# Head mixing on four 64x64 tiles of TensorE: exponentials moved unscaled, with their sums in an extra column, and mixing weights scaled per row by GpSimd

## What is computed

```python
dots = jnp.einsum('bhid,bhjd->bhij', q, k) * scale
attn = jax.nn.softmax(dots, axis=-1)
attn = jnp.einsum('bhij,hg->bgij', attn, reattn_w)      # the head mixing
mean = jnp.mean(attn, axis=1, keepdims=True)            # over the 16 mixed heads
var = jnp.var(attn, axis=1, keepdims=True)
attn = (attn - mean) * jax.lax.rsqrt(var + LN_EPS)
out = jnp.einsum('bhij,bhjd->bhid', attn * gamma + beta, v)
return out @ w_out + b_out
```

## Time and profile before

| | |
|---|---|
| median of 3 runs | 904.35 us (901.05 to 905.14) |
| profiled execution, its own time | 896.37 us |
| span of the profiled execution | 894.6 us |
| mean granted TensorE clock | 0.933 of full speed |
| instructions | 14228 |

### The profile page before, as it was taken

The page is one execution under the profiler, slowest core; times in us unless marked ns, Lnnn a source line. Parts: engine busy times, 40 slices in busy tenths (PEclk is TensorE's granted clock), DMA queues, the critical chain, the costliest instruction groups (busy, mean ns, idle before and its releaser), DMA issues.

```text
span 894.6 us, 14228 instructions
## 1 busy us (share of the span) xinstructions
PE 735.4 (82%) x4514; PEld 525.0 (59%) x4514; DVE 683.3 (76%) x1442; ACT 438.7 (49%) x1198; POOL 180.2 (20%) x367
## 2 busy tenths in 40 slices
PE   2758689988897989898898889898989889788654
PEld 2435466756574757566675667575766567456421
DVE  2587778788968896888878886889788896869444
ACT  1004536564647355744656355735475464646310
POOL 1207123013300242013301231023201330013000
PEclk9869799999998999999998999899999999989877
DMA  8400400140005000321014000410023000500000
GB/s 305 143 0 22 167 25 1 52 138 7 30 3 161 33 29 0 100 87 35 0 38 150 6 29 0 143 51 29 0 84 104 13 1 19 171 7 7 1 7 5
DMA packets 28102, 49.26 MB, mean 55 GB/s; under 512 B 2715, under 2 KB 9124, under 8 KB 27812
## 3 DMA queue, kind: packets, MB, share of 16 engines
q1 hardware_dynamic: 24340, 45.34, 15.2%
q10 hardware_dynamic: 3728, 3.49, 1.2%
HBM read 13.16 MB, written 2.11 MB: 17 GB/s over the span
## 4 chain that ended last, share of the span: by engine, by line
PE 33%; DVE 23%; issue 23%; ACT 8%; POOL 6%; DMA 6%; SPq 1%; POOLq 0%; ACTq 0%; DVEq 0%
PE big L534 5%; PE small L685 5%; PE big L551 5%; DMA pg<-pst 5%; PE small L534 5%; DVE an L1263 4%; PE big L617 4%; DVE pst L1185 3%; ACT pst L917 2%; DVE var L1220 2%; DVE mx L1192 2%; PE small L670 2%; ACT ot L1006 1%; PE big L715 1%; DMA tok_b<-in_tok_b 1%
## 5 line engine op out<-in xcount | busy, mean ns | idle before, releaser
L617 PEld LDWEIGHTS big<-w_mix,pg 128*128 128x128 f32 x1024 | 124.0, 197 | 48.2 <-DVE an L1263 37.4
L617 PE MATMUL big<-w_mix,pg 128*128 128x128 f32 x1024 | 130.9, 285 | 25.2 <-DVE an L1263 23.4
L917 ACT ACTIVATE pst<-big,nb 128x256 f32<-128x256 f32 x256 | 117.9, 474 | 47.2 <-DVE nb L1195 24.0
L1263 DVE TENSOR_TENSOR an<-big,rstd 128x1024 f32<-128x1024 f32 x64 | 131.6, 2057 | 2.8 <-DVE rstd L1250 0.2
L1192 DVE TENSOR_REDUCE mx<-big 128x4 f32<-128x1024 f32 x64 | 78.3, 1223 | 26.4 <-PE big L551 25.8
L938 ACT ACTIVATE sqb<-big 128x1024 f32<-128x1024 f32 x64 | 65.0, 1018 | 58.9 <-PE big L617 58.9
L551 PE MATMUL big<-qk_t 64*128 64x256 f32 x512 | 73.9, 408 | 20.3 <-ACT qk_t L900 20.3
L1220 DVE TENSOR_REDUCE var<-sqb 128x64 f32<-128x1024 f32 x64 | 76.5, 1203 | 0.8 <-ACT sqb L938 0.8
L1185 DVE TENSOR_SCALAR pst<-pst,rr 128x256 f32<-128x256 f32 x256 | 72.8, 349 | 0.0
L551 PEld LDWEIGHTS big<-qk_t 64*128 64x128 f32 x512 | 44.8, 188 | 45.6 <-ACT qk_t L900 27.1
L640 PE MATMUL small<-w_qkv,xnv 128*128 128x512 f32 x128 | 61.7, 605 | 4.0 <-DVE h L1363 4.0
(11 more groups left out here) (200 smaller groups left out, 1224.7 us busy)
## 6 DMA issues: line engine op xcount, KB each, us to landing
pg<-pst SPq DMA_DIRECT2D x128, 256.0 KB
w_qkv<-in_w_qkv SPq DMA_DIRECT2D x1, 3072.0 KB
xt<-in_x_t SPq DMA_DIRECT2D x8, 256.0 KB, 2.9
xr<-in_x_tok SPq DMA_DIRECT2D x8, 256.0 KB, 2.6
out<-h SPq DMA_DIRECT2D x16, 128.0 KB
an<-in_gate_t ACTq DMA_DIRECT2D x1, 1024.0 KB, 9.3
an<-in_up_t ACTq DMA_DIRECT2D x1, 1024.0 KB, 25.1
an<-in_down_t ACTq DMA_DIRECT2D x1, 1024.0 KB, 27.5
```

The lines of the kernel that those rows point to most:

```text
L617: last = mm(mix_place(n)[:, i * P:(i + 1) * P], pg[:, hf * (IB // 2) + i, it * T + jt * P:it * T + (jt + 1) * P], w_mix[:], start=True, st ...
L917: last = A(pst[:, g % 2, h % GH, it, :], big[p % 2][:, (j * TT + it) * T:(j * TT + it + 1) * T], ACT.Exp, bias=nb[:, h, it:it + 1], scale= ...
L1263: V.tensor_tensor(an[:, jt, :, c:c + 64].rearrange("p g c -> p c g"), mix_place(n)[:, :].rearrange("p (c g) -> p c g", g=H), rstd[:, n % 2 ...
```

## The change

- The normalisation of the exponentials on VectorE (`normalise`) goes. `pst` and `pg` become 520 columns wide (`PW`); VectorE adds `sums` and the class token's exponential into columns 512 and 513 of each head's row, pair by pair (`total(p)`), and each DMA carries 514 columns (2056 bytes a row instead of 2048), after `("tot", p)` of its pair instead of after `normalise`. The class token's `dck` and `eck` are also made pair by pair.
- `rows_of(h)` becomes every 16th partition from h on. A partition is again (token of 8, head of 16), but now in that order, so 64 rows hold 4 tokens with all 16 heads.
- VectorE takes the reciprocals of the sums that came with the DMAs (`row_scales`, 128x32), and GpSimd multiplies `w_mix` (now 64 columns, 4 tokens) with them in 4 instructions of 128x512 (`scale_weights`) into `w_rows`, which lies in slot 0 of `pst`.
- A mixing block has 30 matmuls (60 passes) instead of 8 (16 passes): for i = 0 two of 64 rows x 128 weight columns, for i = 1 to 7 four of 64 x 64, each with 64 streamed columns. The two row halves write to the two banks of the PSUM tile. The output's layout is unchanged.
- The permutation of tokens moves into TensorE: `mixer_turn` and `turn_class` become matmuls with permutation matrices `to_place` and `to_token` (two more constants loaded, 64 KB each), and the copies L894 and L1215 become plain.

```diff
-    base = h // GH * QG * GH + h % GH
-    return slice(base, base + (QG - 1) * GH + 1, GH)
+    return slice(h, P, H)
...
-        pst = sb("pst", [P, 2, GH, TT, T])
+        pst = sb("pst", [P, 2, GH, PW])
+        w_rows = pst[:, 0, :, :].rearrange("p j m -> p (j m)")[:, 0:TT * IB * QH * H]\
+            .rearrange("p (t i x) -> p t i x", t=TT, i=IB)
...
                     for j in range(GH):
-                        if j % (GH // 2) == 0:
-                            sp.wait_ge(dve_s.sem, dve_s.at(b, (("p", j // (GH // 2)), g)))
                         h = g * GH + j
-                        sp.dma_start(pg[rows_of(h), :, :], pst[:, g % 2, j, :, :])\
+                        if j % 2 == 0:
+                            sp.wait_ge(dve_s.sem, dve_s.at(b, ("tot", h // 2)))
+                        sp.dma_start(pg[rows_of(h), :, 0:SUM + TT], pst[:, g % 2, j, 0:SUM + TT])\
                             .then_inc(s_sh[g % 2][j // 2], 16)
...
-                        last = nc.tensor.transpose(bank[2][:, c * T + tt * P:c * T + (tt + 1) * P],
-                                                   xn[:, tt, c * P:(c + 1) * P], ident[:])
+                        last = mm(bank[2][:, c * T + tt * P:c * T + (tt + 1) * P],
+                                  xn[:, tt, c * P:(c + 1) * P], to_place[:], start=True, stop=True)
...
+                if jt == 0:
+                    pe.wait_ge(pool_w.sem, pool_w.at(b, (it, hf)))
                 for i in range(IB // 2):
-                    last = mm(mix_place(n)[:, i * P:(i + 1) * P],
-                              pg[:, hf * (IB // 2) + i, it * T + jt * P:it * T + (jt + 1) * P], w_mix[:],
-                              start=True, stop=True)
+                    ib = hf * (IB // 2) + i
+
+                    for half in ((0, P),) if i == 0 else ((0, 64), (64, P)):
+                        j = slice(it * T + jt * P + half[0], it * T + jt * P + half[1])
+                        for k_hi in range(2):
+                            rows = slice(k_hi * 64, k_hi * 64 + 64)
+                            last = mm(mix_place(n)[half[0]:half[1], k_hi * 512 + i * 64:k_hi * 512 + (i + 1) * 64],
+                                      pg[rows, ib, j], w_rows[rows, it, ib, :], start=True, stop=True)
                 last.then_inc(pe_r.sem, 1)
...
+                def total(p):
+                    hs = slice(2 * p, 2 * p + 2)
+                    dve.wait_ge(act_s.sem, act_s.at(b, ("eck", p)))
+                    V.tensor_tensor(pst[:, p // 2 % 2, 2 * (p % 2):2 * (p % 2) + 2, SUM:SUM + TT],
+                                    sums[:, hs, :], eck[:, hs, :], ALU.add).then_inc(dve_s.sem, 1)
...
-                    normalise(g, 0)
-
-                def normalise(g, part):
-
-                    for j in range(part * GH // 2, (part + 1) * GH // 2):
-                        for it in range(TT):
-                            h = g * GH + j
-                            last = V.tensor_scalar(pst[:, g % 2, j, it, :], pst[:, g % 2, j, it, :],
-                                                   rr[:, h, it:it + 1], None, ALU.mult)
-                    last.then_inc(dve_s.sem, 1)
...
+            def row_scales(b):
+
+                for s in s_sh[0] + s_sh[1]:
+                    dve.wait_ge(s, 16 * 2 * (NGRP // 2) * (b + 1))
+                if not is_(b, 0):
+                    dve.wait_ge(pool_w.sem, pool_w.at(b - 1, (TT - 1, 1)))
+                V.reciprocal(rg[:], pg[:, :, SUM:SUM + TT].rearrange("p i t -> p t i")).then_inc(dve_w.sem, 1)
...
+            def scale_weights(b):
+                pool.wait_ge(dve_w.sem, dve_w.at(b, "rg"))
+                for it in range(TT):
+                    for hf in range(2):
+                        ibs = slice(hf * (IB // 2), (hf + 1) * (IB // 2))
+                        G.tensor_tensor(w_rows[:, it, ibs, :], w_mix[:].unsqueeze(1).to_broadcast([P, IB // 2, QH * H]),
+                                        rg[:, it, ibs].unsqueeze(2).to_broadcast([P, IB // 2, QH * H]), ALU.mult)\
+                            .then_inc(pool_w.sem, 1)
```

More of the change, by code:

```diff
@@ L43 @@
 QG = 8
+QH = QG // 2
 IB = P // QG
@@ L47 @@
 AW = T + 2
+SUM = TT * T
+PW = SUM + QG
 CQ, ONE = P, P + 1
@@ L82, in rows_of, with place_of @@
 def rows_of(h):
-    base = h // GH * QG * GH + h % GH
-    return slice(base, base + (QG - 1) * GH + 1, GH)
-def head_of(row):
-    return row // (QG * GH) * GH + row % GH
+    return slice(h, P, H)
+def place_of(token):
+    half, k_hi, i, k_lo = token // 64, token // 32 % 2, token // QH % (IB // 2), token % QH
+    return k_hi * 64 + k_lo * IB + half * (IB // 2) + i
 class Stage:
@@ L305, in build @@
         act_s = stage("act_s", [("q", 0)] + [x for p in pairs for x in
-                      ([("q", p + 1)] if p < HP - 1 else []) + [("e", p)] + ([("eck", p // 2)] if p % 2 else [])
-                      ] + ["eq"])
-        finish = ["tot", "r", "pck", ("p", 0)]
+                      ([("q", p + 1)] if p < HP - 1 else []) + [("e", p), ("eck", p)]] + ["eq"])
+        finish = ["r", "pck"]
         dve_s = stage("dve_s", ["sck", "sq", "mq", "nq"]
                       + [x for p in pairs for x in
[L311 to L315, removed]
+                         [("mx", p), ("nb", p), ("d", p)] + ([("tot", p - 1)] if p else [])
+                         + ([(f, p // 2 - 1) for f in finish] if p and p % 2 == 0 else [])]
+                      + [("tot", HP - 1)] + [(f, NGRP - 1) for f in finish] + ["rq", "pq", "pckt"])
         pool_s = stage("pool_s", ["pcc"])
+        dve_w = stage("dve_w", ["rg"])
+        pool_w = stage("pool_w", [(it, hf) for it in range(TT) for hf in range(2)])
         r_order, sq_order, a_order = [], [("sq", 0), ("ln", 0), ("ex", 0), "qs", "cs", ("sq", 1)], [("v", 0)]
@@ L572, in turn_class @@
                 for it in range(TT):
-                    last = nc.tensor.transpose(bank[2][0:H, it * P:(it + 1) * P], pck[:, it, :], ident[:])
+                    last = mm(bank[2][0:H, it * P:(it + 1) * P], pck[:, it, :], to_token[:], start=True, stop=True)
                 last.then_inc(pe_s.sem, 1)
@@ L893, in mixer_turned @@
                     act.wait_ge(pool_x.sem, pool_x.at(b - 1, "xnv"))
-                A(permuted(xnt[:].rearrange("p c l -> p (c l)")),
-                  bank[2][:, :].rearrange("p (t i k) -> p t i k", i=IB, k=QG), ACT.Copy).then_inc(act_a.sem, 1)
+                A(xnt[:], bank[2][:, :].rearrange("p (c l) -> p c l", c=MC), ACT.Copy).then_inc(act_a.sem, 1)
             def scores(b, before_last=None):
@@ L1207, in scores @@
                         between[p]()
+                total(HP - 1)
                 finish_group(NGRP - 1)
-                normalise(NGRP - 1, 1)
                 dve.wait_ge(act_s.sem, act_s.at(b, "eq"))
@@ L1385, in iteration @@
                 project(b, 1)
-                ffn_x(b, ff, P, 1, (dve_o.sem, dve_o.at(b, ("h3", 1))), lambda: ffn_out(b, ff, P, 0))
+                ffn_stats(b, ff, P, 1, (dve_o.sem, dve_o.at(b, ("h3", 1))))
+                if do_scores:
+                    row_scales(b + 1)
+                ffn_norm(b, ff, P, 1)
+                ffn_quant(b, ff, P, 1)
+                ffn_out(b, ff, P, 0)
                 if do_mixer:
@@ L1490, in _ @@
             mixer_y(1)
+            row_scales(0)
             mixer_out(1)
@@ L1695 @@
         "w_qkv": chunks(x["L0_attn_w_qkv"]).reshape(P, MC, 3 * INNER),
-        "mix_rep": x["L0_attn_reattn_w"][[head_of(r) for r in range(P)]], "mix16": x["L0_attn_reattn_w"],
+        "mix_rep": x["L0_attn_reattn_w"][[r % H for r in range(P)]], "mix16": x["L0_attn_reattn_w"],
         "gamma": np.repeat(x["L0_attn_ln_gamma"], DH).reshape(HP, P).T,
```

56 lines of the change are left out of this document (28 added, 28 removed).

## The result

The changed kernel takes 984.82 us (median of 4 runs, 983.37 to 986.76), the kernel before beside it 902.70 (898.25 to 905.14). The ratio is 1.092, with an interval of 1.087 to 1.097. The forecast was 887 us in a range of 866 to 908: the sign and the range are both wrong.

What follows compares the result with a forecast made beforehand. No engine's share decides: VectorE paces the mixing, TensorE the scores and after. Terms -10.5 - 2.4 - 4 - 1.6 + 1.6 = -17 us from 896.4 give 879 us profiled, 887 us as median; range 866 to 908.

Steps and rivals of the forecast that it cites:

- I take 5.5 us, as the bytes grow by 0.4%: Scores: time from issuing a pair's DMAs to a free slot, assumed unchanged although rows grow to 2056 bytes.
- -10.5 us: Scores: earlier DMAs end ScalarE's slot wait, gaining 1.3 us an image, for 8 images.
- Rival B: Scores: rows of 2056 bytes move at half the rate, the slot wait stays, 902 us; chance 0.10.
- The early issue: Scores: pair 0's DMAs go at 459.0 instead of 463.12, freeing the slot 2.9 us before pair 4 wants it.
- -2.4: Behind the scores: VectorE is free earlier for the token mixer's bias add, 0.3 us of TensorE's short idles an image.
- -4 us: Scores and after: without the wait TensorE's clock drops less, a gain of 0.5 us an image.
- The blocks, 1.62 us forecast: Head mixing: four tiles side by side, a block 0.2 us less than before, -1.6 us in all.
- A: Mixing blocks: small passes are bound by their number, a block takes 2.5 us, 903 us in all; chance 0.10.
- D: Mixing blocks: tiles load and stream one after the other, 4.0 us a block, about 999 us; chance 0.14.
- The permutation: Token permutation in TensorE: copy gain of 0.45 us offset by added passes; turn_class's 2 passes cost +1.6 us.
- The scaling of the weights: nothing: Weight scaling: row_scales costs 0.2 us once cover is gone; GpSimd's 5.1 us is covered by 2.0 us of slack.

Runs made afterwards that it cites:

- e2: The kernel before with only rows_of changed to every 16th partition, so other heads are mixed: 989.84 us, ratio 1.097.
- e7: e6 with only rows_of changed to every 16th partition, so other heads are mixed: 1028.08 us.
- e6: The changed kernel with the old rows_of and 128x128 mixing blocks, weights scaled early and 128 columns wide: 919.90 us, ratio 1.022.
- e1: The kernel before with DMA rows of 514 columns (2056 bytes) at a pitch of 520, nothing else: ratio 0.998.
- e3: The changed kernel with DMA rows of 512 columns at pitch 520, constants standing in for the row sums: 986.82 us, ratio 1.094.
- e9: e6 with 39 one-column memsets at the start of VectorE's program: 906.58 us, ratio 1.006.
- e13: e9 with GpSimd's two weight multiplies for it=0 left in place and the two for it=1 moved into the mixing: 897.39 us, ratio 0.996.
- e4: The changed kernel with row_scales moved behind ffn_quant on VectorE, so GpSimd's multiplies start later: 967.42 us, ratio 1.070.
- e5: The changed kernel with row_scales and scale_weights moved to an earlier gap: 1012.95 us, ratio 1.124.
- e11: e4 with 39 one-column memsets at the start of VectorE's program: 960.12 us, ratio 1.063.
- e8: e5 with each head's partitions 8 apart in both row halves, sent as two DMAs of 4 partitions: 1033.59 us, ratio 1.150.
- e14: e8's rows with e4's late scaling and 39 memsets, the upper half's transfers issued by ScalarE's queue: 983.86 us, ratio 1.088.
- e12: The kernel before with 80 one-column memsets at the start of VectorE's program: 917.27 us, ratio 1.017.

## Why the prediction was wrong

**"I take 5.5 us, as the bytes grow by 0.4%": the step that failed.** The transfers were priced by their bytes, and the only doubt was the row's length. That the diff also changes `rows_of`, from a step of 4 partitions to one of 16, stood in no term, no bound and no rival. The 5.5 us became 13.1. Where -10.5 us was counted, e2 shows +87 for that line alone in before, and e7 against e6 +108. Rival B had the symptom (late transfers) but the wrong cause, which e1 and e3 refute, and stopped at 902 us, because it let the wait only stay and not grow.

**The early issue** was right: 7.65 us behind the stage's begin, 7.9 forecast. With fast packets (e6, e9) the slot wait is gone. But it is worth 1.2 us an image and not the 2.7 that were waited, close to the 1.3 of the forecast: the pace of TensorE's own work sets the stage at 24.3 us.

**"-2.4" behind the scores** did not come: in e9 and e13 the stretch between the gates is 25.6 and 24.3 us, where before has 24.2.

**The clock, "-4 us":** wrong in sign. It is 0.857 in the profiled run of after for 0.933 before, as TensorE waits more; in e13 it is 0.942.

**The blocks, 1.62 us forecast:** 1.41 measured, so A (2.5 us) and D (4.0 us) are out. D's time of 999 us is near the result, but its mechanism is refuted: 60 passes in 1.41 us leave 24 ns for each, less than the 57 ns that 64 columns cost by themselves. In the trace a group of four passes follows every 58 ns, the 0.057 us of the forecast; what came out smaller is the rest of the block, 0.6 us for 0.83. That a faster block is worth little while VectorE sets the pace was right.

**The permutation** came as forecast: the plain copy of `xnt` takes 0.60 us, the matmuls in its place 1.16 instead of 0.66.

**"The scaling of the weights: nothing": the second step that failed.** GpSimd's time was right (4.13 us for 5.1 forecast), and so was its own cover. What was not asked is what VectorE does meanwhile. Each of three steps on SBUF alone ends about 0.15 us behind the end of one of GpSimd's multiplies: 2.2 us more in a chain, 17 us of the run (e4). `row_scales` was counted at 0.2 us with "its DMAs have landed long before"; it took 0.35, and with slow transfers it waits for them as soon as it stands earlier (e5).

The Trainium skill, "SBUF — State Buffer", Who interferes with whom, has the rule: where VectorE needs the ports that it shares with GpSimd (a tensor_scalar in a two-port mode, or two operands in SBUF), the one that comes later waits until the other has ended. The trace agrees: in e6 `th` took 2.24 us instead of 0.69 and ended 0.55 us behind a multiply, and the next multiply was the longer one.

**What no step of mine named:** the loop of VectorE moved to a place where it is fetched anew. It cost 7 us in the changed kernel (e11 against e4) and 13 in e6.

Together: e4 and e11 take 25 us of the 82 away. The 57 us left are less than the 87 and 108 us that the step of 16 costs by itself, so the other parts of the change give something back beside it; how much each of them gives there was not measured. Whether a four-tile form can beat before stays open. It would need three things at once: the rows of a head in both halves of the partitions, fast packets, and eight of them under way. The step of 4 lacks the first, the step of 16 the second, the split transfers of e8 and e14 the third.

## What to carry to other kernels

Price a transfer by where its rows land, not by its bytes: list the destination partitions before and after a layout change, and measure one such transfer before building on it. When work is moved to GpSimd, look up what VectorE does on SBUF in that stretch, in both orders, and put the work beside steps that read PSUM or wait anyway. After any edit compare the page's instruction packets: a loop that was held and is now fetched costs some us at each jump, whatever the edit was about.

## What was not expected of the hardware

- The same transfer of 256 KB to 8 partitions has packets of 84 ns with the partitions 4 apart and of 171 ns with 16 (e2), with about eight packets under way in both.
- Two queues with transfers to 4 partitions each have 4.5 packets under way together, no more than one queue has (4.4; e14 and e8).
- 39 memsets of one column ahead of a loop made a kernel 13 us faster (e9), 80 made another 15 us slower (e12).
- Four 64x64 tiles with 64 streamed columns take 58 ns for four passes, in float32, with the weights of each pass loaded beside it.
- A VectorE step of 0.2 us with its operands in SBUF takes 1.2 us beside a multiply of GpSimd (`rstd` in e13), and GpSimd's next multiply can be held up in turn (2.35 us for 1.90, e6).
